# Products of the identity with itself, unread, where a play-through leaves TensorE without a part

## What is computed

```python
xn = _layernorm(x, axis=-1)
x = x + _L0_attn_ref(xn, ...) + _L0_ffn_ref(xn, ...)   # causal softmax attention, 16 heads of 8;
                                                      # 16 experts of 64 (top 2) + a shared one of 128
xn = _layernorm(x, axis=-1)
x = x + _L1_attn_ref(xn, ...) + _L1_ffn_ref(xn, ...)   # delta rule, one step per token, 16 heads of 8;
                                                      # 4 usable experts of 704 (top 2)
```

```python
state = state * (1.0 - bb * kk) + bb * (vt[..., :, None] * kt[..., None, :])
out_t = jnp.einsum('bhij,bhj->bhi', state, qt)
```

## Time and profile before

| | |
|---|---|
| device time, median of 3 runs (lowest to highest) | 2012.01 us (1992.42 to 2012.99) |
| the profiled execution: device time, span | 2013.11 us, 2011.4 us |
| mean granted TensorE clock (1 is 2.4 GHz, 0.5 is 1.2 GHz) | 0.865 |
| instructions in the trace | 29786, of them 9764 matrix products |

### The profile page before, as it was taken

The page is one execution under the profiler, slowest core; times in us unless marked ns, Lnnn a source line. Parts: engine busy times, 40 slices in busy tenths (PEclk is TensorE's granted clock), DMA queues, the critical chain, the costliest instruction groups (busy, mean ns, idle before and its releaser), DMA issues.

```text
span 2011.4 us, 29786 instructions
## 1 busy us (share of the span) xinstructions
PE 1567.2 (78%) x9764; PEld 967.2 (48%) x9766; DVE 1395.0 (69%) x2664; ACT 978.3 (49%) x1600; POOL 905.1 (45%) x973
## 2 busy tenths in 40 slices
PE   2953977898777998888654887999999988698950
PEld 2840444454444554444332554656666655465530
DVE  5775655676555776776677855788888878787822
ACT  2721545565444665445444544556665644455410
POOL 4247437725543224658786265111111257621126
PEclk9875979998776999778776888999999989999985
DMA  6954678888655765656445374565665657665423
GB/s 207 291 150 140 197 196 232 246 224 225 193 163 169 207 176 139 160 151 191 114 130 183 111 214 151 162 187 172 172 185 170 185 181 230 200 179 167 131 80 90
DMA packets 277946, 354.44 MB, mean 176 GB/s; under 512 B 32272, under 2 KB 204304, under 8 KB 272416
## 3 DMA queue, kind: packets, MB, share of 16 engines
q1 hardware_dynamic: 237600, 287.92, 50.4%
q0 software_dynamic: 17056, 33.66, 5.8%
q10 hardware_dynamic: 23136, 30.94, 4.5%
HBM read 197.48 MB, written 122.68 MB: 159 GB/s over the span
## 4 chain that ended last, share of the span: by engine, by line
PE 43%; DVE 15%; issue 14%; ACT 8%; POOL 6%; DMA 5%; SPq 4%; another core or an unknown queue 4%; ACTq 0%; DVEq 0%; POOLq 0%
PE Y L1062 7%; PE R L819 5%; PE R L821 5%; PE R L820 5%; PE R L835 3%; POOL xs_dram L1368 3%; DVE state L2024 3%; PE Y L957 3%; PE R L922 2%; ACT probs L1535 2%; PE R L895 2%; DVE row_max L1923 2%; DVE acc_in L1749 2%; DVE dw L2018 2%
## 5 line engine op out<-in xcount | busy, mean ns | idle before, releaser
L1923 DVE TENSOR_REDUCE row_max<-R 128x6 f32<-128x768 f32 x256 | 241.3, 953 | 133.3 <-PE R L922 65.8
L1388 POOL TENSOR_TENSOR o_acc<-o_acc,read 128x512 f32<-128x512 f32 x112 | 143.9, 1284 | 408.4 <-DVE read L2034 407.5
L1368 POOL DMA_INDIRECT xs_dram<-sc_in,pos x256 | 269.4, 1052 | 109.5 <-issue 63.6
L1347 POOL DMA_INDIRECT gat<-ys_dram,pos x256 | 253.8, 992 | 133.2 <-issue 68.0
L1379 POOL TENSOR_SCALAR_AFFINE_SELECT probs<-probs 128x512 f32<-128x512 f32 x256 | 167.7, 655 | 316.6 <-ACT probs L1535 312.6
L1062 PE MATMUL Y<-hid,fd 128*128 128x512 f32 x456 | 250.0, 630 | 35.2 <-DVE hid L2072 26.5
L1535 ACT ACTIVATE probs<-R 128x768 f32<-128x768 f32 x256 | 205.0, 808 | 137.6 <-PE R L945 91.9
L819 PE MATMUL R<-fhl,fw 128*128 128x512 f32 x418 | 231.8, 555 | 19.2 <-issue 5.1
L2072 DVE TENSOR_TENSOR hid<-R,sil 128x512 f32<-128x512 f32 x228 | 155.7, 686 | 60.1 <-ACT sil L1654 24.4
L2024 DVE TENSOR_TENSOR_SCAN state<-dw 128x512 f32<-128x512 f32 x128 | 172.3, 1346 | 16.2 <-issue 7.9
L1654 ACT ACTIVATE sil<-R 128x512 f32<-128x512 f32 x190 | 112.9, 595 | 140.1 <-PE R L821 103.0
(11 more groups left out here) (270 smaller groups left out, 3479.7 us busy)
## 6 DMA issues: line engine op xcount, KB each, us to landing
fw<-wf SPq DMA_DIRECT2D x38, 1408.0 KB
q_rows<-kq SPq DMA_DIRECT2D x128, 256.0 KB
fx<-xs_dram SPq DMA_DIRECT2D x86, 256.0 KB
xs_dram<-gat SPq DMA_DIRECT2D x24, 512.0 KB, 4.6
qk_dram<-qk_parts SPq DMA_DIRECT2D x32, 384.0 KB
Q<-qk_dram SPq DMA_DIRECT2D x64, 192.0 KB
K<-qk_dram SPq DMA_DIRECT2D x64, 192.0 KB
fw<-wf SPq DMA_DIRECT2D x96, 128.0 KB
```

Of the source, the lines that this page charges most:

```text
L1347: pool.indirect_dma_start(gat[:, i % 2, 2 * t + a, :], None, ys_dram[l][g], bass.IndirectOffsetOnAxis(ap=pos[l][g][a][:, col:col + 1], axi ...
L1368: pool.indirect_dma_start(xs_dram[g], bass.IndirectOffsetOnAxis(ap=pos[l][g][a][:, col:col + 1], axis=0), sc_in[:, n % 2, t * P:(t + 1) * ...
L1923: dve.tensor_reduce(row_max[:, b, h2, :, :], pair[:, :].rearrange("p (g c t) -> p g c t", g=2, t=P)[:, :, 0:3, :], AX.X, ALU.max).then_inc ...
```

## The change

In the play-through, when TensorE is free and no ready stage fits, and parts for it are still to come, a *filler* is now put into TensorE's list, from time 20.0 on. It takes no part in the dependencies and is assumed to last 0.22 us. A ready stage that comes up during it waits for its end in the play-through. A filler also needs an empty bank of ring `R` and takes the one that has been empty for longest. In the kernel, a filler is a wait for the release of that bank by its last user, and one bf16 product of the 128 x 128 identity (stationary) with the identity repeated four times (128 x 512, moving). Nothing reads what it writes. The first filler also waits for the constants of VectorE (`consts_v`), among them the identity in bf16.

```diff
     RINGS = {"R": 7, "Y": 1}
     SIGNAL = 0.12
+    FILLER, FILL_FROM = 0.22, 20.0
 
     def __init__(self):
         self.parts, self.index, self.takes, self.frees, self.ends, self.last = [], {}, {}, {}, {}, {}
@@ -161,12 +163,16 @@
             return True
 
         ready, busy, result = {e: [] for e in ENGINES}, dict.fromkeys(ENGINES, False), {e: [] for e in ENGINES}
+        fillers, unfilled = [], sum(part[1] == "PE" for part in self.parts)
         events = [(start[i], 0, i) for i in range(len(names)) if not missing[i]]
         while events:
             now = min(events)[0]
             due = sorted(event for event in events if event[0] <= now)
             events = [event for event in events if event[0] > now]
             for _, done, i in due:
+                if i < 0:
+                    busy["PE"] = False
+                    continue
                 t, e = self.parts[i][:2]
                 if not done:
                     ready[e].append((t, i))
@@ -190,11 +196,21 @@
                         certain.add(i)
                         result[e].append(names[i][:3])
                         events.append((now + self.parts[i][2], 1, i))
+                        unfilled -= e == "PE"
                         break
+                else:
+                    empty = [b for b, h in enumerate(held["R"]) if h is None]
+                    if e == "PE" and not busy[e] and unfilled and empty and now >= self.FILL_FROM:
+                        busy[e] = True
+                        fillers.append(("FILL", len(fillers), 0, min(empty, key=lambda b: since["R"][b])))
+                        result[e].append(fillers[-1][:3])
+                        events.append((now + self.FILLER, 1, -1))
         left = [name for i, name in enumerate(names) if missing[i]]
-        assert sum(map(len, result.values())) == len(names), left[:8]
-        return result, {names[i][:3]: [chosen[i, j] for j in range(len(self.takes.get(i, ())))]
-                        for i in range(len(names)) if self.parts[i][1] == "PE"}
+        assert sum(map(len, result.values())) == len(names) + len(fillers), left[:8]
+        places = {names[i][:3]: [chosen[i, j] for j in range(len(self.takes.get(i, ())))]
+                  for i in range(len(names)) if self.parts[i][1] == "PE"}
+        places.update((filler[:3], [filler[3]]) for filler in fillers)
+        return result, places
 
 
 def table():
@@ -842,6 +858,16 @@
             for kind, n, k in ORDER["PE"]:
                 par = n % 2
                 places = iter(BANKS[kind, n, k])
+                if kind == "FILL":
+                    if n == 0:
+                        pe.wait_ge(consts_v, CONSTS_V)
+                    b = next(places)
+                    if users["R"][b]:
+                        pe.wait_ge(*users["R"][b].released())
+                    users["R"][b] = None
+                    pe.matmul(psum["R"][:, b * C:(b + 1) * C], ident_b[:, :],
+                              ident_b[:, :].unsqueeze(1).to_broadcast([P, TILES, P]), start=True, stop=True)
+
                 if kind == "A1":
                     if n == 0:
                         pe.wait_ge(consts, CONSTS)
```

## The result

The changed kernel takes 2034.57 us, the median of four runs (2023.45 to 2044.53); the kernel before, with one more run, 2006.68 us (1992.42 to 2012.99). The ratio is 1.0147, with a 95% interval of 1.0101 to 1.0194: slower by 1.5%, where 0.8% was forecast. It lies among the times over 2032 us, which had a chance of 0.36; within 1% had 0.41. The profiled execution took 2033.93 us, with a span of 2032.2 us.

A forecast was written before the change was run, and what follows sets the result against it. TensorE was taken as busiest, with half the share of the end time and 375 us of short stalls for fillers; 1 + 2 + 6 + 2 - 5 + 10 = +16 us gave a median of 2028 us, 8-in-10 range 1980 to 2072.

The forecast's parts named there:

- the second forecast: 100 to 205 us, 188 fillers: TensorE's lateness can be hidden by an unknown wait; +2 us, bounds -5 and +12.
- The start: 0 to 100 us, 40 fillers: first router product 6 us late, partly regained by a higher clock or hidden; +1 us.
- the unknown wait of 17.62 us: 100 to 205 us: a wait in the chain that ended last, said to be able to hide TensorE's lateness.
- From 205 to 793 us: 205 to 800 us, 61 fillers: half of 13 us on the path, clock unchanged; +6 us, bounds 0 and +26.
- At 1100 us: 1070 to 1200 us: fillers fill the stall for `kl`, experts start up to 10 us sooner; -5 us, other bound +15.
- the third rival: Shifted order costs by itself: fillers and `FT1` ahead of `D2`, scan loses 15 us, or 30: 2042 us; chance 0.12.
- From 1201 us on: 1200 to 1942 us, 219 fillers: a third on the path +16, clock -6; together +10 us, bounds -10 and +35.
- Half an us at the end for each us of work on TensorE: Whole kernel: an us more TensorE work, where it is not idle, is worth about half an us at the end.
- The signs named beforehand: TensorE: 10546 instructions, busy time up 170 to 250 us, clock over 0.9 from 800 to 1200 us, gap at 1075 filled.
- The term behind it: Higher clock takes 21 us of work off from 800 to 1070 us and 11 us from 1200 to 1942 us.
- the signs against the forecast: 205 to 800 us over 20 us longer, fillers waiting for banks, scan waiting over 10 us for `D2`, or clock over 0.95.
- The clock rival: 793 to 1202 us: 122 us of work rises from 1.2 GHz, fillers hide in stalls; 1972 us, chance 0.23 for over 1% faster.

The follow-up runs named there:

- e11: The changed kernel, unaltered, measured once more on chip 10: 2037.55 us against 2006.41 for the kernel before, ratio 1.0154.
- e12: The changed kernel without its first 228 fillers, 552 kept, on chip 10: 2020.07 us, ratio 1.0075 to the kernel before.
- e5: The changed kernel, unaltered, on chip 3: 1942.70 us against 1940.16 for the kernel before, ratio 1.0010.
- e1: The changed kernel's lists and banks with all 780 fillers left out: 1938.06 us against 1942.41 for the kernel before, ratio 0.9964.
- e2: The kernel before, its order unchanged, with 620 fillers put into idle spans of its play-through: 1935.67 us, ratio 0.9973 to the kernel before.
- e9: The kernel before with 86 more DMA copies of 256 KB on SP's queue, on chip 10: 2010.15 us, ratio 1.0011 to the kernel before.
- e3: The changed kernel with every filler twice, 1560 products: 2009.88 us, ratio 1.0341 to the kernel before.
- e8: The changed kernel with every filler of 256 columns instead of 512: 1935.58 us, ratio 0.9972 to the kernel before.

## Why the prediction was right, and where not

The sign, and the size within a factor of two, were right: forecast +16 us, measured +28 in the medians and +20.8 between the profiled executions. That the size came out so near is in part luck, since the terms behind it did not hold. By place:

| place | forecast | first measurement | e11 |
|---|---|---|---|
| to `A3` of chunk 12 | +1 | +1.7 | +2.5 |
| to chunk 1 | +2 (-5 to +12) | +19.6 | +16.3 |
| to 793 us | +6 | -6.4 | 0.0 |
| to 1072 us | +2 | +1.7 | +0.1 |
| to 1201 us | -5 | -3.2 | -4.0 |
| to the end | +10 | +7.6 | +10.0 |

Three things about this table. The run of 21 fillers belongs to the second forecast, but its time is in the first row: `A3` of chunk 11, ahead of it, starts 2.5 us earlier than before (96.0 and 98.5). In the same way the run of 11 ahead of `D1` of chunk 2 was counted behind it, so 182 fillers, not 171, stand in the fourth stretch and 90 in the fifth. And single stages move within their neighbourhood: the first `FC1` of tiles 3 and 6 is 0.7 us late and 0.7 us early, that of tile 4 between them 13.3 late.

*The start.* The first filler waited for the constants and then the chunk found a higher clock, as worked out. The timeline of TensorE in the changed kernel:

```profile
34.51 2.74 PE L868 MATMUL R<-ident_b 128*128 128x512 bf16 x6 [34.51 <-DVE K L1802]
...
41.70 0.36 PE L835 MATMUL R<-w0h,xhl 128*128 128x16 f32 x1
41.91 0.26 PE L836 MATMUL R<-w0h,xhl 128*128 128x16 f32 x1
42.03 0.26 PE L837 MATMUL R<-w0l,xhl 128*128 128x16 f32 x1
```

The first router product starts 2.8 us later than before, not 6. The small products are 0.11 to 0.12 us apart instead of 0.21. By chunk 11 the phase is level or better, and the run of 21 then costs 4 us.

*From 100 to 205 us: the step that failed.* The argument was that TensorE's lateness hides behind the unknown wait of 17.62 us. It did not: this stretch took 19.6 us more, and `B1` of chunk 1 was 21.2 us late. The timeline of TensorE shows what it did instead:

```profile
107.44 6.50 PE L868 MATMUL R<-ident_b 128*128 128x512 bf16 x20
...
117.53 9.23 PE L868 MATMUL R<-ident_b 128*128 128x512 bf16 x42
...
171.95 4.55 PE L868 MATMUL R<-ident_b 128*128 128x512 bf16 x18
...
189.74 0.59 PE L868 MATMUL R<-ident_b 128*128 128x512 bf16 x1 [1.05 <-issue]
191.83 0.58 PE L868 MATMUL R<-ident_b 128*128 128x512 bf16 x1 [1.49 <-issue]
193.93 0.59 PE L868 MATMUL R<-ident_b 128*128 128x512 bf16 x1 [1.51 <-issue]
```

and in windows of the changed kernel and of e12, 100 to 215 us:

```profile
100.00:215.00 115.00, 83.59 (x419) 38.47 (x418) 59.26 (x99) 17.32 (x35) 54.19 (x56) 0.78 0.42 122
...
100.00:215.00 115.00, 62.88 (x405) 33.57 (x403) 71.56 (x124) 26.47 (x48) 69.91 (x74) 0.60 0.53 152
```

The first row of the timeline begins with its window and shows 20 of the 21 fillers. All 63 ahead of chunk 13 take 16.1 us, and `A3` of that chunk starts at 126.4 us instead of 118.2, 8 us late. Then most of the `B1`s stand behind 14 to 18 fillers each, 3 to 4 us of work, which is the gap that the play-through leaves between them. A TensorE that arrives late cannot catch up, since it has to work through them first. And from 180 us on its fillers themselves come only one in 1 to 2 us, with "issue" ahead of each: there the real `B1`s wait behind products that nobody reads. TensorE is busy 84 us with the fillers and 63 without, at a clock of 0.78 against 0.60, and every other engine gets less done. In e11 these "issue" pieces are missing and a wait of 17.26 us for ACT stands there instead; the delay is nearly the same. So that part of it is not shown to be their doing.

Being unable to catch up is not the whole cause, for e5 has the same lists. There the last `B1` of chunk 0 starts 16.2 us later than in e1 (183.8 and 167.6), the first of chunk 1 only 9.3, since TensorE waits for POOL in between, and at the end nothing is left of it. There a wait took up part of the lateness, as the forecast argued. On chip 10 the last `B1`s of chunk 0 fall behind a stall of ACT that lasts until 203.5 us (e11), while e12 has issued them all by 183.6. Why the stall is there is not shown.

*From 205 to 793 us*, +6 was forecast and -6.4 and 0.0 measured. The lateness falls to 5.4 us at chunk 3 and is 15.5 at chunk 8. In e12 it goes from -10.4 to -0.6 between the same places, so this rise needs no early fillers. Whether the order or the 61 fillers bring it is not shown. *At 1100 us* the term was right, for a reason only half right:

```profile
1090.47 11.82 PE L868 MATMUL R<-ident_b 128*128 128x512 bf16 x54
1105.67 1.11 PE L851 MATMUL R<-ident,fx 128*128 128x128 f32 x4 [3.38 <-DMA fd<-in_L_ffn_w_dram]
1106.58 3.19 PE L868 MATMUL R<-ident_b 128*128 128x512 bf16 x7
1116.34 0.79 PE L1049 MATMUL R<-kh,pick 128*128 128x512 f32 x1 [6.57 <-DVE kl L2031]
```

The fillers are over before `kl` is there, so they cost nothing, and `FT1` waits 3.38 us for a transfer, inside the same stall. (Before, seven `D2`s stood ahead of `FT1`, not the six of the forecast.) The second to eighth `D2` of the chunk start 32 to 48 us later, as the third rival had it, but by chunk 5 the first `D2` is 4.1 us ahead of before: the experts went first instead. For the other chips e1 shows that this order as a whole is 0.4% faster.

*From 1201 us on*, +10 was forecast and +7.6 measured, but for another reason. The fillers were to cost it. The times between the same stages, in us, say otherwise:

| from the first `FC1` of | before | e2: old order, fillers | changed | e11 | e12 | e1: new order, no fillers | e5 |
|---|---|---|---|---|---|---|---|
| tile 12 to tile 21 | 180.4 | 179.2 | 189.5 | 187.3 | 187.1 | 187.1 | 188.2 |
| tile 21 to tile 24 | 60.9 | 60.4 | 71.2 | 71.4 | 71.3 | 63.1 | 63.5 |
| tile 24 to the last `FZ1` | 314.7 | 297.5 | 314.1 | 314.0 | 315.3 | 298.6 | 299.1 |

Each column is one trace. In the first row the two of the old order agree within 1.2 us (e9, on chip 10, has 180.3), and those of the new order lie 7 to 10 over them, with or without fillers and on either kind of chip. So the shifted order costs this piece, and the fillers at most 2 us of it. In the second row 8 us more come on the slower chips with the changed lists. Whether the order or the fillers bring them is open, since e1 did not run there. The forecast gave the order no term here, and none in attention, where it gained. That the sum came out is luck.

"Half an us at the end for each us of work on TensorE" did not hold as one number: 106 us more on TensorE cost 9 us (e5 against e1), 107 us more cost 28 in the first measurement, and only the 136 us of the second product of each filler cost 67 (e3 against e5, 2009.9 and 1942.7).

*The signs named beforehand.* Right were the 10546 instructions, the gap at 1075 us filled with 54 and 7 fillers, and the longer stretches after 1200 us. Wrong was the busy time of TensorE: up by 107 us, not by 170 to 250. The term behind it was mis-sized: the forecast let the clock take 21 + 11 = 32 us off the real products, and they lost 124. Of the signs against the forecast, fillers did wait for banks (42 us ahead of line 868 besides the first wait, 15.9 of them for `fz`), and the second `D2` at 1100 us came 16 us after the first, where it had been 1 us.

*The clock rival* failed although the clock rose as it said, to 0.87 and 0.93 in the stretches where it was to win. The busy time fell by even more than the 60 us it needed. The time did not follow. What the rise was worth by itself no run shows, for the fillers that raised it are work too. In e2 and e8 it reached 0.925 and 0.923 and the ratio was 0.997, as in e1 with 0.889. From 100 to 205 us the clock went from 0.62 to 0.77. By the rule of the Trainium skill ("TensorE: Matmul & The Clock Gate", on what is actually happening with the clock gate) activity releases the throttle; the trace agrees, with products that nobody reads.

## What to carry over

Work put into idle places of a planned order is free only where the engine arrives in time: ahead of a dense run it takes away the means to catch up. Whether the lateness stays depends on the waits behind it: it was 17 us to the end on one chip and nothing on two others. An edit that also shifts the order needs a run with the order alone, for here the order gained in one place and cost in another, whatever the fillers did. A higher granted clock is not a gain in itself; ask whether the stretches in which it rises end on that engine. And measure such a change on more than one chip: 1.0010 and 1.0154 are the same two kernels.

## What the runs showed of the hardware

Chips 11 and 3 ran the kernel before in 1942 and 1940 us, chip 10 in 2006, 3% more. The engines' own instructions do not account for it: `row_max` takes 241.1 us for 256 in e5 and in the first measurement, and the scan 1404 ns in e5 and 1352 in the first measurement, longer on the faster chip. Of the waits of TensorE, ACT and DVE, 387 us have no visible cause in the trace of the slower kind, and 20 to 28 us in those of the faster, but the former lacks a third of the signals of landed DMAs. With full DMA engines (1.03) three engines were nearly idle for 11 us in the changed kernel there, and not in e5. And 86 copies of 256 KB more, 22.5 MB read and 22.5 MB written on top of 354 MB moved, cost 0.1% (e9), within what could be measured.
